# Value products behind the next scores at both ends of an attention phase, and the first batch's side work one or two units ahead

## The reference

```
x = x + attention(layernorm(x))   # 16 heads of 32; key j banned for query i if j >= 4 and j < i - 128
x = x + experts(layernorm(x))     # 4 experts by token id, each token through one of them, 512 wide
x = x + ffn(layernorm(x))         # silu(bit_linear gate) * bit_linear up, rms norm, bit_linear down, 2048 wide
```

## Time and profile before

| | us |
|---|---|
| median of 3 runs | 785.86 |
| lowest, highest | 783.3, 787.12 |
| the profiled execution | 789.38 |
| its span, first to last instruction | 787.3 |

### The profile page before, as it was taken

One profiled execution on the slowest core, in us unless ns is written; L12 is line 12 of the kernel. 1 busy time (PEld: TensorE's weight loads), 2 busy tenths in 40 slices (PEclk: granted clock), 3 DMA queues, 4 the chain that ended last, 5 costly groups with the idle time before them and its releaser, 6 DMA issues.

```text
span 787.3 us, 14189 instructions
## 1 busy us (share of the span) xinstructions
PE 735.5 (93%) x5167; PEld 512.7 (65%) x5184; DVE 587.4 (75%) x1099; ACT 473.1 (60%) x1028; POOL 331.2 (42%) x329
## 2 busy tenths in 40 slices
PE   5988999999999999999987989999998999999993
PEld 4866777777777776777764777888874444444441
DVE  6986866886667866766665548878888999999882
ACT  4565666766676665766666314444455787667761
POOL 2011205213242134254553544445546677777661
PEclk9998999999999999999999999999999999999997
DMA  9300012214130322314311356555430233333231
GB/s 314 115 1 27 28 40 95 92 44 151 40 107 29 108 85 77 108 31 153 129 40 55 54 198 258 182 197 201 140 126 25 54 88 87 94 95 102 73 92 42
DMA packets 55474, 78.33 MB, mean 99 GB/s; under 512 B 36335, under 2 KB 38383, under 8 KB 53680
## 3 DMA queue, kind: packets, MB, share of 16 engines
q1 hardware_dynamic: 46336, 51.99, 20.6%
q0 software_dynamic: 8784, 24.93, 9.8%
q10 hardware_dynamic: 288, 0.52, 0.2%
HBM read 56.92 MB, written 17.59 MB: 95 GB/s over the span
## 4 chain that ended last, share of the span: by engine, by line
PE 62%; DVE 20%; issue 8%; ACT 5%; POOL 2%; DMA 1%; another core or an unknown queue 0%; ACTq 0%; SPq 0%; POOLq 0%; DVEq 0%
PE side_ps L889 17%; PE pT_ps L976 10%; PE e_z_ps L1528 7%; PE y_ps L1528 7%; PE pv_ps L998 5%; PE s_ps L948 5%; DVE h L1784 4%; ACT hq L1739 2%; DVE neg_max L724 2%; DVE hw_max L1800 2%; DVE hq_big L1831 2%; PE s_ps L956 2%; PE pT_ps L889 1%; DVE probs L745 1%; ACT f_gate L1746 1%
## 5 line engine op out<-in xcount | busy, mean ns | idle before, releaser
L548 ACT ACTIVATE probs<-s_ps,neg_max 128x512 f32<-128x512 f32 (+2 forms) x256 | 152.5, 611 | 17.9 <-DVE neg_max L724 16.4
L724 DVE TENSOR_REDUCE neg_max<-s_ps 128x2 f32<-128x1024 f32 (+2 forms) x128 | 124.6, 1015 | 36.1 <-PE s_ps L956 35.0
L976 PE MATMUL pT_ps<-ident,probs 128*128 128x128 f32 x832 | 116.5, 282 | 7.8 <-DVE probs L745 7.0
L560 ACT ACTIVATE probs<-pT_ps 128x512 f32<-128x512 f32 x96 | 57.5, 599 | 98.7 <-PE pT_ps L976 97.3
L976 PEld LDWEIGHTS pT_ps<-ident,probs 128*128 128x128 f32 x832 | 95.1, 145 | 23.0 <-DVE probs L745 9.7
L745 DVE COPY probs<-pT_ps 128x512 f32<-128x512 f32 x112 | 76.8, 685 | 39.1 <-PE pT_ps L976 36.2
L1695 POOL TENSOR_TENSOR xg_own<-h,ln_w_sb 128x512 f32<-128x512 f32 x63 | 81.9, 1308 | 37.9 <-DVE h L1784 37.8
L889 PE MATMUL side_ps<-w_hi 128*128 128x512 f32 x172 | 71.0, 413 | 0.0
L412 POOL TENSOR_TENSOR aT_hi<-norm,one_col 128x512 fp32r<-128x512 f32 x15 | 15.6, 1041 | 126.6 <-DVE norm L736 88.4
L889 PE MATMUL side_ps<-w_hi,w_lo 128*128 128x512 f32 x172 | 67.5, 392 | 0.0
L889 PE MATMUL side_ps<-w_lo,w_hi 128*128 128x512 f32 x172 | 67.0, 390 | 0.0
(11 more groups left out here) (290 smaller groups left out, 1779.4 us busy)
## 6 DMA issues: line engine op xcount, KB each, us to landing
w_piece<-w_ffn SPq DMA_DIRECT2D x24, 512.0 KB
w_stage<-w_ffn SPq DMA_DIRECT2D x12, 1024.0 KB
xres<-x POOLq DMA_DIRECT2D x4, 1024.0 KB, 6.4
xn<-x SPq DMA_DIRECT2D x3, 1024.0 KB
x<-xres POOLq DMA_DIRECT2D x3, 1024.0 KB, 4.8
xn<-c SPq DMA_DIRECT2D x2, 1024.0 KB, 5.1
v_next<-c SPq DMA_DIRECT2D x2, 1024.0 KB, 7.5
xn<-x SPq DMA_DIRECT2D x4, 256.0 KB, 3.4
```

Source lines behind the costliest of these rows:

```text
L548: nc.scalar.activation(weights[qt][:, h, at:at + width(qt)], s_ps[:, h, 0:width(qt)], ACT.Exp, bias=neg_max[:, qt % 2, h:h + 1], accum_out ...
L560: nc.scalar.activation(out, turned_p, ACT.Identity).then_inc(slot_copied[0], 1)
L724: nc.vector.tensor_reduce(neg_max[:, qt % 2, 2 * s:2 * s + 2], s_ps[:, 2 * s:2 * s + 2, 0:width(qt)], AX.X, ALU.max, negate=True).then_inc ...
L976: last = nc.tensor.transpose(pT_ps[:, k % 2, h * P:h * P + P], weights[qt][:, h, a:z], ident[:])
```

## The change

Three things are done. `values_late` names pairs whose value products are issued one unit later: behind the next unit's scores and its slots 0 and 1. These are, in the last batch, both pairs of groups 1 and 2 and the first pair of group 3, and in batch 0 the second pair of group 0 and both of group 1. ScalarE gets waits on `heads_done` for them, before the exponentials of tile 3 and tile 1, and `heads_done` now counts pairs. VectorE's `attn_of` goes behind its copy of slot 1 where the pair before it is late. Second, in batch 0 the side work is ahead: Q3 and K3 at (0,1,0) and (0,1,1) instead of (0,1,2) and (0,1,3), V0 at (0,1,3), V1 to V3 each a unit ahead or more, X0 to X3 at (0,1,1) to (0,2,0) instead of (0,1,3) to (0,2,2); (0,1,2) and (0,3,1) have no projection. Third, two blocks of routing steps on VectorE move from the end of unit (0,0,3) behind units (0,1,0) and (0,1,1).

```diff
+        FIRST_ROUND = "Q3 K3 X0 X1 V0 X2 V1 X3 V2 V3 Q0 K0 Q1 K1 O0 Q2 K2 O1".split()
         PROJECTED = ("V3 Q2 K2 -", "O2 O3 Q3 K3", "V0 V1 V2 Q0", "K0 V3 Q1 K1", "O0 Q2 K2 O1")
+        FIRST_PROJECTED = PROJECTED[:1] + ("Q3 K3 - V0", "V1 V2 V3 Q0", "K0 - Q1 K1") + PROJECTED[4:]
         TURNED = {(1, 3): "X0", (2, 0): "X1", (2, 1): "X2", (2, 2): "X3"}
+        FIRST_TURNED = {(1, 1): "X0", (1, 2): "X1", (1, 3): "X2", (2, 0): "X3"}
...
+        def values_late(b, g, pair):
+
+            return (b == BATCH - 1 and 1 <= g < HG and (g, pair) != (HG - 1, 2)) or b == 0 and (g, pair) in ((0, 2), (1, 0), (1, 2))
+
+        def values_of(b, g, pair):
+            return 2 * (b * HG + g) + (2 if pair else 1)
...
             def exps(b, g, qt, s):
                 act.wait_ge(max_ready, units_before(b, g, qt) * 2 + s + 1)
+                if s == 0 and qt == 3 and values_late(b, g, 0):
+                    act.wait_ge(heads_done, values_of(b, g, 0))
+                if s == 0 and qt == 1 and g and values_late(b, g - 1, 2):
+                    act.wait_ge(heads_done, values_of(b, g - 1, 2))
...
-                dve.wait_ge(heads_done, b * HG + g + 1)
+                dve.wait_ge(heads_done, values_of(b, g, 2))
...
-                if qt == 0 and 0 < g < HG:
+                follows_late = qt == 0 and 0 < g < HG and values_late(b, g - 1, 2)
+                if qt == 0 and 0 < g < HG and not follows_late:
                     attn_of(b, g - 1)
...
                 copy_slot(b, g, qt, 1)
+                if follows_late:
+                    attn_of(b, g - 1)
...
-            for qt, route_parts in enumerate(((tiles_needed, rows_started), (slots_given,), (), (slots_addressed, experts_of_tiles))):
+            for qt, route_parts in enumerate(((tiles_needed, rows_started), (slots_given,), (), ())):
...
+                        if (b, g, qt) == (0, 1, 0):
+                            slots_addressed()
+                        if (b, g, qt) == (0, 1, 1):
+                            experts_of_tiles()
...
-                if pair:
-                    last.then_inc(heads_done, 1)
+                last.then_inc(heads_done, 1)
...
                 transpose_slot(b, g, qt, 0)
                 transpose_slot(b, g, qt, 1)
+                if qt == 2 and values_late(b, g, 0):
+                    attend_pair(b, g, 0)
+                if qt == 0 and g and values_late(b, g - 1, 2):
+                    attend_pair(b, g - 1, 2)
...
-                if qt % 2:
+                if qt % 2 and not values_late(b, g, qt - 1):
                     attend_pair(b, g, qt - 1)
```

More of the change, by code:

```diff
@@ L232, in round_of @@
         def round_of(b, kinds):
-            names = AHEAD if b < 0 else [n for n in IN_ROUND if taken(b, n)]
+            names = AHEAD if b < 0 else FIRST_ROUND if b == 0 else [n for n in IN_ROUND if taken(b, n)]
             return [n for n in names if n[0] in kinds]
@@ L247, in projected @@
         def projected(b, g, qt):
-            name = PROJECTED[g].split()[qt]
+            name = (PROJECTED if b else FIRST_PROJECTED)[g].split()[qt]
             return None if name == "-" or (g and not taken(b, name)) else name
         def turned(b, g, qt):
-            return TURNED.get((g, qt)) if b < BATCH - 1 else None
+            return (TURNED if b else FIRST_TURNED).get((g, qt)) if b < BATCH - 1 else None
         def batch_of(b, name):
@@ L857, in vector_program @@
                     part()
-            assert done[0] == ROUTE_STEPS
             def batch(b, last):
@@ L863, in batch @@
                         unit(b, g, qt, last)
+                        if (b, g, qt) == (0, 1, 0):
+                            slots_addressed()
+                        if (b, g, qt) == (0, 1, 1):
+                            experts_of_tiles()
+                            assert done[0] == ROUTE_STEPS
                         if (b, g, qt) == (0, 1, 2):
```

## The result

The changed kernel takes 791.28 us (median of 7 runs, 790.76 to 793.61) against 784.9 us for the kernel before (7 runs, 782.66 to 787.12): a ratio of 1.0086, 95% interval 1.0069 to 1.0102. That is 6.4 us or 0.86% slower, outside the range of 781.0 to 790.0 and on the side that had a chance of 0.12.

What follows compares the result with a forecast made beforehand. TensorE bounds the middle of attention; a loop over TensorE, VectorE and ScalarE sets the pace at both ends. First batch +0.5 and last batch −0.9 sum to −0.4 us, giving 785.5 from a median of 785.86; range 781.0 to 790.0.

Steps and rivals of the forecast that it cites:

- X0 behind K3: First batch, unit (0,1,1): X0 waits 2.6 us for K3's low half, slot 3 before it 1.2.
- Its price: First batch in all: −0.4 us at the full clock, +1.3 with it down; +0.5 taken.
- Where V3 goes: To (0,3,1) before; without V3 that 7.66 us unit takes about 6.95, only 0.7 of the projection's 2.8 coming back.
- Late values, last batch: Last batch: worth 0.2 us a group by themselves; with two clock falls taken, −0.9 us.
- (a): Last batch, unit qt=0: scores, slots, values, hand-over, exponentials; next scores at 6.55 us, a gain of 0.45.
- (b): Last batch, unit qt=1: loses the values at its end; 4.5 us, before 6.54, or 6.1 at the full clock.
- (c): Last batch, unit qt=2: scores, slots, values of pair 0, hand-over, exponentials; 5.5 us against 4.02.
- (d): Last batch, unit qt=3: exponentials done at 4.94 us, next scores at 5.05.
- ScalarE's wait: Last batch: exponentials of tiles 1 and 3 wait for late values sharing their weights' storage; no size of its own.
- Rival 1: Slower by clock falls on TensorE's work ahead of exponentials, qt=0 and qt=2, up to 1.6 us each; 791.9 us; chance 0.12.
- Rival 2: X0 doesn't wait for K3: first batch −3.0, last −1.7 or better, 781.2 to 780 us; chance 0.18.
- Rival 3: The change moves nothing that counts, values and clock falls as before: 785.9 us, within 1.5; chance 0.22.

Runs made afterwards that it cites:

- the single pair: Only the side work moved ahead, plus the first pair of (0,1) late: 788.61 us, ratio 1.0028 to before, 3.0 us over side work alone.
- changed with storage apart: The changed kernel with weights of tiles 2 and 3 stored apart from tiles 0 and 1, so no ScalarE waits: 786.03 us, ratio 1.0002 to before.
- the other two: Only the side work moved ahead, plus the last pairs of groups 0 and 1 of batch 0 late: 786.12 us, ratio 1.0003 to before.
- the pair back: The changed kernel with the first pair of (0,1) back at the end of its unit, between K3 and X0: 789.51 us, ratio 1.0044 to before.

## Why the prediction was wrong, point by point

- **What bounds the ends:** right. The loop of scores, maxima and exponentials sets the pace, and the values only move between two of its parts.
- **X0 behind K3:** right in place and size. Added up: next scores 9.8 us after those of (0,1,2), a wait of 2.6 us, 1.2 ahead of slot 3. Measured 9.90, 2.41 and 0.57.
- **Its price: the step that failed.** The prediction's own sum gave a first batch of −0.4 at the full clock and +1.3 with it down, and then took the middle, +0.5. Measured 4.4, with the same work coming back later (2.3 us, predicted 2.2). The 3.2 us between 98.2 and what was measured, on the same zero, are: 1.3 in (0,1,0), where the low clock lasted over the transposes and 1.8 us went into what was put at 0.8; 0.9 in (0,1,2), where the clock stayed low for 6.8 us, not the 3.4 of each fall in the attention phase of before; 0.1 and 0.2 in the units around; and 0.8 in (0,2,0), whose steps add up to 8.4 us, not 7.6. Each low stretch was put at half rate on the scores or at 1.6 us, at even odds; the two in this execution cost more. Nor was the chance even: of the five profiles in which X0 waits over 2 us, four have the low clock behind it (changed, the single pair, late values of batch 0 alone, changed with storage apart), and in the profile before a fall stood behind every wait of over 1.5 us. But it is no rule: with the routing steps back, 2.38 us of waiting brought none.
- **Where V3 goes:** right. Its old unit fell from 7.65 to 6.81 us, 0.8 of the projection's 2.8.
- **Late values, last batch: mis-sized and of the wrong sign.** −0.9 predicted, +1.3 timed. Of the four terms two were short: (a) 6.55, measured 6.95; (b) 4.5, 4.53 where the clock held; (c) 5.5, 5.93; (d) 5.05, 5.12. The four add up to 22.5 us at the full clock, not 21.6. In (a) the miss is in the small steps of TensorE: the eight transposes ahead of the values take 0.98 us, not the 0.80 that they took ahead of a projection, and the values 1.84 with both sink products, not 1.63; the two are the 0.4 us. The 21.8 for the old order was right: its four units where the clock held, in other profiles, are 5.82, 6.11, 4.02 and 5.91. So the new order loses 0.7 us a group before any fall, where 0.2 of gain was predicted: 1.8 of the miss of 2.2 over two groups. A margin of 0.2 us a group was smaller than the errors of the terms it was made of.
- **ScalarE's wait:** named as what takes the gain, and not priced by itself. It costs 5.1 us, more than all else in the last batch. Giving the two pairs' weights room of their own was a question to ask at that point.
- **The rivals.** Rival 1 gave 791.9 for a loss by the clock, from five falls in the last batch; the time is near it, the way there isn't. Falls in the last batch were two in the profile of changed, fewer than before, and the harm was in the first batch. Rival 1's place and price are real all the same: in the four other profiles with this last batch a fall hits the unit (3,3,0) and makes it 8.4 to 8.5 us instead of 6.96. Rival 2 fell with the wait of 2.41 us. Rival 3 fell in both parts.
- **Not foreseen: 1.5 us behind attention,** below.

Do the parts add up? By the timed medians and ratios against before: side work ahead −0.8, the pair (0,1) first +3.0 (0.0038 of ratio), the other two +1.0, the last batch +1.3: 4.5 us, where changed shows 6.8 by its ratio. With the pair back it is 3.5 where the parts say 1.5. The 2 us left over are no more than the intervals of the four or five ratios allow together (each is 0.9 to 1.8 us either way). Whether late values of batch 0 and of the last batch cost more together stays open; nothing in the code ties the two.

## What to carry to other kernels

Before moving work out from between a producer and a consumer of the same bank, ask what it hid: here the value products covered the way of K3 through two engines, and their place mattered more than the order of all the side work. If two orders at the full clock differ by less than the errors of the terms, count the ties instead: a new wait of one engine on another in a loop with no slack is a cost, and storage apart may buy it off. And where a long wait comes out of the sum, put the low clock behind it in at a whole price from rows, over every step that it can reach, and take its chance from more than one execution.

## What the runs showed of the hardware

**A VectorE operation four times as long beside GpSimd.** One multiplication in the third phase, of 128x512 float32 from SBUF to SBUF, takes 0.48 us before, and in the two kernels that leave batch 0 as before. In the other 11 it takes 1.95 to 1.98 us, once, at the same step of the work or one near it, and the rest of the kernel is 1.2 to 1.7 us longer (340.7 against 341.9 to 342.4). Before:

```profile
598.54 0.48 DVE L1206 TENSOR_SCALAR xq_big<-f_xn,x_inv 128x512 f32<-128x512 f32 x1
```

```profile
598.70 1.45 POOL L1695 TENSOR_TENSOR xg_own<-h,ln_w_sb 128x512 f32<-128x512 f32 x1
```

changed:

```profile
599.18 1.96 DVE L1230 TENSOR_SCALAR xq_big<-f_xn,x_inv 128x512 f32<-128x512 f32 x1
```

```profile
598.35 2.50 POOL L1719 TENSOR_TENSOR xg_own<-h,ln_w_sb 128x512 f32<-128x512 f32 x2
```

GpSimd runs two such operations one behind the other in both. Before, the first ends at 598.67 and VectorE's begins 0.13 us ahead of that; it is done at 599.02, and GpSimd's second takes 1.45 us instead of 1.27. In changed both of GpSimd's take 1.27 us, back to back from 598.35 to 600.85; VectorE's begins 0.44 us ahead of the end of the first, and ends 0.3 us behind the second. The Trainium skill ("SBUF — State Buffer", section "SBUF: two separate sides") says that VectorE, in some of its operations, and GpSimd share a pair of ports as an exclusive lock, and that the loser of the two waits through the other's whole instruction. The rows agree with it in kind, one held up while the other runs, but they show more than one instruction of waiting: VectorE's was held over what was left of the first and the whole of the second. Why every kernel with another batch 0 meets GpSimd a few tenths of a microsecond earlier in its operation here, 500 us later, was not tested.

**The same wait, with and without a fall.** Behind unit (0,0,3)'s work, ahead of a transpose of the sinks' weights, TensorE waits 2.17 or 2.18 us in all 14 profiles (the wait ends between 56.2 and 58.4 us). In nine of them the clock stands at 1.2 GHz within 3 us of its end, for 3.4 us or, in two, 6.8; in five it doesn't fall there. The first batch of changed took 84.57 us and that of the kernel with the routing steps back 79.47, at ratios of 1.0086 and 1.0068: of the 5.1 us between them 0.8 are the routing steps, and most of the rest is the low clock. One profile is enough for the length of a wait, and not for the time of a stretch in which the clock may fall.
